# Placing SBUF buffers on one phase modulo 128 bytes, and one maximum ahead of a query column, in a two-block cross-attention kernel

## The reference

```python
# block 0: L=512 tokens x of width 512, S=1024 context rows, 32 query heads on 8 key/value heads of 16
q, k, v = x @ Wq + bq, ctx @ Wk + bk, ctx @ Wv + bv
x = layernorm(softmax(q k^T / 4 + mask) v @ Wo + bo + x) * gamma + beta
# block 1: two cross-attention layers on the same context, 16 heads of 128, then a feed-forward part
for i in (1, 2):
    h = layernorm(x)
    q, k, v = h @ wq + bq, ctx @ wk + bk, ctx @ wv + bv        # 512 -> 2048 each
    k, v = concat(k, bias_k), concat(v, bias_v)                # one more key and value
    x = x + softmax(q k^T / sqrt(128)) v @ wo + bo
x = x + gelu(layernorm(x) @ w_fc1 + b_fc1) @ w_fc2 + b_fc2     # 512 -> 2048 -> 512
```

## Time and profile before

| what | value |
|---|---|
| median of 3 runs (lowest to highest) | 2689.46 us (2682.36 to 2690.98) |
| the profiled execution: time, span of its instructions | 2688.83 us, 2687.0 us |
| granted TensorE clock, mean | 0.994 of full speed |
| busy share of the span: TensorE, weight loads, VectorE, ScalarE, GpSimd | 98%, 80%, 64%, 56%, 49% |
| block 0 (with its projections), first layer's loop | about 0 to 291 us, about 341 to 740 us |

### The profile page before, as it was taken

One profiled execution on the slowest core, in us unless ns is written; L12 is line 12 of the kernel. 1 busy time (PEld: TensorE's weight loads), 2 busy tenths in 40 slices (PEclk: granted clock), 3 DMA queues, 4 the chain that ended last, 5 costly groups with the idle time before them and its releaser, 6 DMA issues.

```text
span 2687.0 us, 48709 instructions
## 1 busy us (share of the span) xinstructions
PE 2621.7 (98%) x17432; PEld 2142.9 (80%) x17432; DVE 1717.0 (64%) x2630; ACT 1506.4 (56%) x2350; POOL 1320.1 (49%) x750
## 2 busy tenths in 40 slices
PE   7999999999999999998999999999999999999989
PEld 6777788888888888886877777888888888888867
DVE  6999765655656655664279996665565665666541
ACT  4999555545445555444459994555545555554533
POOL 1244246665544666554603433466556456655633
PEclk9999999999999999999999999999999999999989
DMA  7411024354423445441462110335445134535411
GB/s 187 108 49 66 33 71 122 96 127 121 103 66 85 108 108 128 107 117 61 149 139 92 57 59 33 96 96 127 121 103 128 34 97 114 132 98 122 113 63 63
DMA packets 88385, 261.80 MB, mean 97 GB/s; under 512 B 20112, under 2 KB 33696, under 8 KB 81840
## 3 DMA queue, kind: packets, MB, share of 16 engines
q1 hardware_dynamic: 88240, 259.80, 37.1%
HBM read 135.45 MB, written 6.83 MB: 53 GB/s over the span
## 4 chain that ended last, share of the span: by engine, by line
PE 78%; DVE 7%; ACT 5%; issue 4%; SPq 2%; DMA 2%; POOL 1%; ACTq 0%; DVEq 0%; POOLq 0%
PE ps_t L1009 17%; PE ps_m L1009 17%; PE ps_s L1009 12%; PE ps_m L1253 6%; PE ps_t L1133 6%; PE ps_t L1253 5%; PE ps_m L1148 5%; PE ps_s L1117 4%; PE ps_m L1133 3%; ACT p L811 2%; DVE nmx L1658 2%; SPq L412 2%; PE ps_m L1186 1%; DMA pT<-pb 1%; DVE pb L1677 1%
## 5 line engine op out<-in xcount | busy, mean ns | idle before, releaser
L498 POOL TENSOR_TENSOR pT<-pT,pT 128x1024 fp32r<-128x1024 f32 x224 | 538.7, 2406 | 508.4 <-ACT pT L685 507.5
L685 ACT ACTIVATE pT<-pT 128x1024 fp32r<-128x1024 f32 x224 | 237.9, 1062 | 355.5 <-DMA pT<-pb 355.5
L811 ACT ACTIVATE p<-ps_s,nm 128x1024 f32<-128x1024 f32 x256 | 284.3, 1111 | 255.3 <-DVE nm L1661 254.9
L1009 PE MATMUL ps_s<-kT,qT 128*128 128x512 f32 x1536 | 395.2, 396 | 12.6 <-ACT p L811 8.5
L1677 DVE STREAM_TRANSPOSE pb<-p 128x1024 f32<-128x1024 f32 x224 | 278.3, 1243 | 114.3 <-ACT p L811 107.2
L1009 PEld LDWEIGHTS ps_s<-kT,qT 128*128 128x128 f32 x1536 | 278.5, 188 | 84.2 <-ACT p L811 24.3
L1658 DVE TENSOR_REDUCE nmx<-ps_s 128x1 f32<-128x1024 f32 x256 | 309.7, 1210 | 40.8 <-PE ps_s L1009 40.7
L1585 DVE CUSTOM_DVE_ANT_0 sm<-ps_s,mask 128x1024 f32<-128x1024 f32 x256 | 309.8, 1211 | 6.8 <-PE ps_s L1117 4.4
L767 ACT ACTIVATE p<-sm,nm 128x1024 f32<-128x1024 f32 x256 | 294.2, 1149 | 33.6 <-DVE nm L1585 30.2
L1009 PE MATMUL ps_t<-ctxT,wa 128*128 128x512 f32 x1080 | 262.2, 396 | 0.0
L1009 PE MATMUL ps_m<-hT,wa 128*128 128x512 f32 x1008 | 250.1, 399 | 3.6 <-ACT g L971 3.5
(11 more groups left out here) (144 smaller groups left out, 4460.6 us busy)
## 6 DMA issues: line engine op xcount, KB each, us to landing
pT<-pb SPq DMA_DIRECT2D x896, 128.0 KB, 2.4
stg_qk<-in_wqk SPq DMA_DIRECT2D x40, 1024.0 KB, 7.5
stg_vo<-in_wo SPq DMA_DIRECT2D x48, 512.0 KB, 3.5
wob<-in_wo SPq DMA_DIRECT2D x32, 512.0 KB, 3.6
stg_vo<-in_wv SPq DMA_DIRECT2D x32, 512.0 KB, 3.6
q_stack<-scr_q SPq DMA_DIRECT2D x48, 128.0 KB, 4.2
st_ctx<-in_ctxT SPq DMA_DIRECT2D x8, 512.0 KB, 5.9
bv_row<-scr_bv SPq DMA_DIRECT2D x32, 128.0 KB, 5.8
```

The source lines that it names most:

```text
L498: return nc.gpsimd.tensor_tensor(out, x, f32(hi), ALU.subtract)
L685: return nc.scalar.activation(out, in_, ACT.Copy)
L811: nc.scalar.activation(p[t % 2][:], ps_s[t % 2][:], ACT.Exp, bias=nm[:, i:i + 1], scale=SCALE1, accum_out=sums[:, i:i + 1]).then_inc(exp_d ...
L1009: mm = nc.tensor.matmul(out, lhs(x, c), rhs(y, c), start=start and c == 0 and i == 0, stop=stop and c == n_tiles - 1 and i == 2)
```

## The change

There are two parts.

**Placement.** The offset at the start and the offset at `region` are rounded up to 128 bytes; the first was at a multiple of 128 before, and stays. Block 0's buffers begin 128 bytes behind `region`, block 1's at `region`. The value weights leave `wa` for a buffer pair `wv` of their own, with 32 bytes ahead of it and 96 behind. Phases after: `ctxT`, `hT`, `ident` 0; everything behind `region` 0, with `wv` alone at 32 (a few small buffers of block 0 aside). So weights `wa` stand on the phase of `hT` and `ctxT`, where they stood 96 bytes above it (which modulo 128 is 32 below); the value weights stand 32 above `ctxT`, where they stood 96 above; `p` stands on the phase of `ident`, where it stood 96 above; `kT` with `qT`, `pT` with `v`, `wo` with `cT` and with `gT` were on one phase and still are.

**Order.** In every body VectorE runs `maxima(9)` ahead of `lo_column` of head 1's query block. In the first body of a layer ScalarE takes quarter 2 of the moved probabilities behind `hi_column` of that block, and quarter 3 behind `exp(9)`.

```diff
-        start = (nc.sbuf_base + 31) // 32 * 32
+        start = (nc.sbuf_base + 127) // 128 * 128
...
+        at[0] = (at[0] + 127) // 128 * 128
         region = at[0]
+        at[0] += 128
         q_stack = sb("q_stack", [STACK, NH0, L], BF16)
...
         at[0] = region
-        wa = sb("wa", [P, 3, CT, 256], F32R, 2)
+        wa = sb("wa", [P, 2, CT, 256], F32R, 2)
+        at[0] += 32
+        wv = sb("wv", [P, CT, 256], F32R, 2)
+        at[0] += 96
         wo = sb("wo", [P, 2, D], F32R, 2)
...
                         hi_column(n + K0[1], 1, 0, k_half(0, 1))
-                        hi_moved(x, (0, 1, 2) if first else (1, 2, 3))
+                        hi_moved(x, (0, 1) if first else (1, 2, 3))
                         exp_moved(8, x + 1)
                         hi_column(n + Q1, 0, 1, q_all(1))
                         if first:
+                            hi_moved(x, (2,))
+                        exp_moved(9, x + 1)
+                        if first:
                             hi_moved(x, (3,))
-                        exp_moved(9, x + 1)
...
-                                        lambda q, c: wa[q][:, 2, c, :], CT)
+                                        lambda q, c: wv[q][:, c, :], CT)
...
                         maxima(8)
+                        maxima(9)
                         lo_column(n + Q1, F_Q1, 0, 1, q_all(1))
-                        maxima(9)
                         blocks(8, x + 1)
```

More of the change, by code:

```diff
@@ L506, in lo_v @@
                 pool.wait_ge(vo_hi, use + 1)
-                flat = wa[1][:, 2].rearrange("p c n -> p (c n)"), wa[0][:, 2].rearrange("p c n -> p (c n)")
-                lo(flat[0], stg_vo[:].rearrange("p s n -> p (s n)"), flat[1]).then_inc(vo_lo, 1)
+                flat = [w[:].rearrange("p c n -> p (c n)") for w in wv]
+                lo(flat[1], stg_vo[:].rearrange("p s n -> p (s n)"), flat[0]).then_inc(vo_lo, 1)
             def lo_o(use, w=wo):
@@ L698, in split_v @@
                 act.wait_ge(vo_in, 16 * (use + 1))
-                copy(wa[0][:, 2].rearrange("p c n -> p (c n)"), stg_vo[:].rearrange("p s n -> p (s n)"))\
+                copy(wv[0][:].rearrange("p c n -> p (c n)"), stg_vo[:].rearrange("p s n -> p (s n)"))\
                     .then_inc(vo_hi, 1)
```

## The result

| kernel | median (runs) | profiled span |
|---|---|---|
| before | 2687.7 us (2682.4 to 2691.0, 4 runs) | 2687.0 us |
| changed | 2647.2 us (2645.7 to 2648.9, 4 runs) | 2645.5 us |

The ratio is 0.9856, with a 95% interval of 0.9844 to 0.9868: the changed kernel is faster by 40.5 us, where I had forecast 21.4.

A forecast was written before the change was run, and what follows sets the result against it. TensorE, busy 98% of the span, was taken to bound the kernel through matmul cadence and small waits. Order 12.1 plus query/key placement 9.3 made 21.4 us off 2688.8: forecast 2667.5 us, range 2649 to 2680.

The forecast's parts named there:

- The place and kind of the stall: Loop turns: tile 11 waits for `exp(9)`, 0.43 us removable; in first bodies `values` then waits for GpSimd.
- Order in all: 12.1 us: Attention loops: new VectorE and ScalarE order saves 10.3 us in turns and 1.8 us in first bodies.
- I take 230.0: Query and key matmuls `hT,wa` and `ctxT,wa`: aligned, they fall from 234.2 and 233.3 to 230.0 ns, saving 9.3 us.
- `kT,qT`, `wo,cT` stay where they are: Matmul pairs already on one phase: their cadence, 226.7 to 231.7 ns, does not change.
- Value weights: I take no change: 3072 value matmuls of 256 columns: off phase before and after, they stay at 118.3 ns.
- rival 1: Value matmuls gain too, to 114 ns, 14.3 us more: 2653 us; chance 0.22.
- The sum itself: Whole kernel: order's 12.1 and placement's 9.3 us simply add to 21.4 us off.
- 2 (placement does nothing): Cadence differences belong to the operands, so only the order gains: 2676.7 us; chance 0.11.
- Rivals 3: Value matmuls lose half of the cadence spread, 3.75 ns each, 11.5 us: 2679 us; chance 0.08.
- 4: Another VectorE or GpSimd wait takes the order's gain in every turn: 2679.5 us; chance 0.05.
- 5: Slower: value matmuls' weight loads and moving columns clash more at 32 above, 2690.4 to 2713 us; chance 0.04.
- the transposes: Transposes (`p` against `ident`) change phase but stay at 109 ns; no gain or loss taken.

The follow-up runs named there:

- e6_wa_32: The changed kernel with `wa` too at 32 bytes above `hT` and `ctxT`, `wv` left 32 above: 2666.1 us, ratio 0.9925 against the kernel before.

## Why the prediction was wrong in size

**The place and kind of the stall: right.** Tiles 10 and 11 run as one, `nmx` starts 0.04 us behind the scores, the cover is 1.3 us, `values` waits for GpSimd in first bodies. 0.46 us a turn, 0.43 forecast.

**"Order in all: 12.1 us": mis-sized.** Order alone measured 18.9 us. The turns and the first stall came as counted (11.0 and 1.8 us for 10.3 and 1.8). What failed is that nothing else was counted: the second half of the first bodies (3.1 us) and the last pairs (2.3 us). Part of it stood in the list of waits as 0.8 us for GpSimd's `pT` at L1253, which I did not follow, and the labels understate it: `exp` and GpSimd were down for 8.5 + 0.8 us there, and twice that came back. The length of whole stretches would have shown it: scores to scores, a first body took 57.6 to 58.5 us where the others took 56.4.

**"I take 230.0": mis-sized.** `hT,wa` and `ctxT,wa` came to 228.0 and 227.4 ns, near the lower bound of 226.7, and gave 5.8 + 8.2 = 14.0 us where I had 9.3; some 0.8 of it is in 144 matmuls of `hT,wa` at other lines, which my 1008 left out. The 230 came from a mixture. `kT,qT` and `wo,cT` had two cadences in the earlier trace rows, 226.7 and 230 to 231.7, and both pairs were aligned in both places. What differed is the run ahead: before, `kT,qT` in a turn took 232.1 ns behind `hT,wa` and 226.7 behind `wo,cT`; after, behind `hT,wa`, 228.3, with its last interval counted, which belongs to the load of `wa`. So an aligned pair's own cadence is 226.7, and the slow rows carried something over from an unaligned neighbour. That also was missing as a term of its own: "`kT,qT`, `wo,cT` stay where they are" was wrong by 1.8 + 1.5 = 3.3 us.

**"Value weights: I take no change": wrong by 4.0 us.** 117.2 ns and not 118.5 (118.3 in the row): between my case and rival 1 (114). The rival's side was the right one and its size not; and with `wa` unaligned only half of it comes (117.9 in `e6_wa_32`). That they stood "96 above before" was true modulo 128 and hid that they stood 32 below modulo 256; in neither reading did a row of before say which was better.

**The sum itself.** I added order and placement. Measured, placement is worth 10.3 us alone and 19.5 behind the order: with the old order more than half of the 22.6 us that it gives in cadence was waited away for `exp(9)`, whose chain from the DMA-fed quarter on is 6.24 us at either cadence. My sum took placement's cadence in full, which is right only because the order was changed with it, and I did not say so. Of the rivals, 2 (placement does nothing) is refuted by the order-only kernel, 19.5 us above both together, and by placement alone, whose interval ends at 0.9974. The two independent ports that the Trainium skill tells of ("TensorE: Matmul & The Clock Gate", "Step-by-step: what each phase is for") can't alone describe this: the same load behind the same columns takes 227.4 or 233.1 ns by 32 bytes of address. Rivals 3, 4 and 5 did not come.

**The account.** 12.1 + 9.3 = 21.4 us forecast. In the traces it is 18.8 of stalls and 14.0 + 3.3 + 4.0 + about 1.3 of cadence, 41.5 in all but for rounding; the medians say 40.5. The 1.3 has 0.9 for the transposes, which I had put at nothing; but between kernels of one placement they differ as much (114.0 to 115.0 ns), so no part of it is shown to be theirs.

**What stays open.** Why a distance of 32 or 128 costs 5 to 6 ns, and why for 256 columns 32 above is best and 0 nearly the worst, no run tells. The last interval of a run is settled above; what an unaligned run leaves behind in the next one, and by which operand, is not. `pT,v`, at distance 0 in all kernels, stayed at 233.5 ns; its columns lie in scattered pieces, and that was not varied.

## What to carry to other kernels

Where TensorE is busy all the time, measure the distance from start to start for each pair of operands, and vary the distance of their buffers modulo 256 bytes: 0 was best of those tried for 512 columns of fp32r and not for 256, so each kind wants its own try. Count the weights of the next run as a pair with the operand that moves now. A faster engine is worth its gain only where no chain of other engines ends behind it; take such a wait away first, or price the two edits together. To find it, look for a stretch of other engines' work that keeps its length (6.24 us here) while TensorE's changes. Count stalls by the length of stretches that should be equal, not by the list of waits: its labels made 9.3 us of one whose removal brought 18.9.

## What was new of the hardware

- The cadence of 512-column fp32r matmuls with a 128x128 load each goes by the distance of the loaded weights from the moving buffer modulo 256 bytes: 227.4 to 228.0 ns at 0 (also at 256), 233 at 32 on either side, 232.5 at 128. All buffers 32 bytes up left the five main cadences within 0.2 ns.
- The load that counts is the one in flight: the last interval of a `kT,qT` run is 226.7 ns where the next run's weights are aligned with `kT`, 232.4 where they are 128 off, and 236.7 at 96 below.
- For the value matmuls, 256 columns of `wv` moving past a loaded tile of `ctxT`, the order is another: with `wv` 32 above `ctxT` 117.2 ns (117.9 beside an unaligned `wa`), at 64 118.0, at 32 below 118.5, at 0, 96 and 128 120.1 to 120.3.
- A run is slowed by the one ahead of it: the first five intervals of the same `kT,qT` took 232.0 ns behind an unaligned `hT,wa` and 227.5 behind the same run aligned.
